# Routed rows gathered by an adding indirect DMA straight into the residual, eight groups ahead

## What is computed

```
x = x + _L0_xattn_ref(_layernorm(x), ctx, W, b)
x = x + _L0_ffn_ref(_layernorm(x), gate_w, shared and routed weights)
x = x + _L1_xattn_ref(_layernorm(x), ctx, ctx, Wq, bq, Wk, bk, Wv, bv)
x = x + _L1_ffn_ref(_layernorm(x), W_in, b_in, W_out)
```

```
top_id = jnp.argmax(x @ gate_w); score = jax.nn.sigmoid(top_val)
y = silu((x*score) @ rt_gate[e]) * ((x*score) @ rt_up[e]) @ rt_down[e]
routed = y of expert top_id;     return shared + routed
```

## Time and profile before

| | us |
|---|---|
| median of 3 runs | 897.83 |
| lowest and highest | 892.91, 898.03 |
| span of the profiled execution | 890.3 |
| TensorE busy in it | 821.5 |
| VectorE busy | 650.6 |
| ScalarE busy | 545.3 |
| GpSimd busy | 250.1 |

### The profile page before, as it was taken

One profiled execution on the slowest core, in us unless ns is written; L12 is line 12 of the kernel. 1 busy time (PEld: TensorE's weight loads), 2 busy tenths in 40 slices (PEclk: granted clock), 3 DMA queues, 4 the chain that ended last, 5 costly groups with the idle time before them and its releaser, 6 DMA issues.

```text
span 890.3 us, 15056 instructions
## 1 busy us (share of the span) xinstructions
PE 821.5 (92%) x4236; PEld 618.0 (69%) x4277; DVE 650.6 (73%) x1695; ACT 545.3 (61%) x947; POOL 250.1 (28%) x328
## 2 busy tenths in 40 slices
PE   4899998887589969999999999999999999999997
PEld 2677776666556746667777777777777777777775
DVE  3677778876574326587788888878887888788774
ACT  2365566555333313536777777787877687777765
POOL 1112112177717725012033213321321232131000
PEclk9899999999799989999999999999999999999999
DMA  5236575453235424210000000000000000000000
GB/s 143 58 93 166 157 212 154 126 143 112 81 93 154 133 74 121 71 47 22 4 25 24 18 6 24 24 7 17 24 24 0 24 24 24 0 24 13 13 1 24
DMA packets 91421, 55.66 MB, mean 63 GB/s; under 512 B 13439, under 2 KB 88183, under 8 KB 91255
## 3 DMA queue, kind: packets, MB, share of 16 engines
q1 hardware_dynamic: 74304, 40.38, 16.1%
q0 software_dynamic: 4096, 8.40, 3.3%
q10 hardware_dynamic: 12983, 6.41, 2.5%
HBM read 32.10 MB, written 23.07 MB: 62 GB/s over the span
## 4 chain that ended last, share of the span: by engine, by line
PE 62%; POOL 10%; DVE 9%; issue 7%; ACT 6%; DMA 3%; ACTq 1%; another core or an unknown queue 1%; DVEq 0%; POOLq 0%; SPq 0%
PE PS L742 7%; PE PS L987 7%; PE PS L1009 6%; PE PS L1011 6%; PE PS L1010 6%; PE PS L988 6%; PE PS L989 6%; POOL x_sorted L497 5%; PE PS L998 4%; PE PS L760 3%; POOL rs L482 2%; PE PS L996 2%; PE PS L923 2%; POOL xs L490 2%; DVE xn L1069 2%
## 5 line engine op out<-in xcount | busy, mean ns | idle before, releaser
L697 ACT ACTIVATE sil<-PS,b_in_c 128x512 f32<-128x512 f32 x256 | 161.9, 684 | 112.4 <-PE PS L996 68.1
L1374 DVE TENSOR_TENSOR sil_l<-sil,sil_h 128x512 fp32r<-128x512 f32 x256 | 164.7, 684 | 44.9 <-ACT sil_h L705 44.2
L480 POOL TENSOR_TENSOR ve<-mv,eps 128x4 f32<-128x4 f32 x64 | 17.3, 271 | 504.8 <-DVE mv L1063 504.7
L705 ACT ACTIVATE sil_h<-sil 128x512 fp32r<-128x512 f32 x224 | 128.9, 631 | 0.0
L1009 PE MATMUL PS<-sil_h,wout_l 128*128 128x512 f32 x256 | 121.4, 474 | 1.7 <-DVE sil_l L1374 1.7
L1358 DVE TENSOR_SCALAR dec<-PS,b_in_c 128x512 bf16<-128x512 f32 x128 | 95.4, 745 | 25.3 <-PE PS L989 25.3
L987 PE MATMUL PS<-x4T_h,win_l 128*128 128x512 f32 x256 | 102.5, 400 | 0.9 <-ACT sil L697 0.4
L1011 PE MATMUL PS<-sil_h,wout_h 128*128 128x512 f32 x256 | 100.6, 393 | 0.0
L1010 PE MATMUL PS<-sil_l,wout_h 128*128 128x512 f32 x256 | 100.5, 393 | 0.0
L988 PE MATMUL PS<-x4T_l,win_h 128*128 128x512 f32 x256 | 99.8, 390 | 0.0
L989 PE MATMUL PS<-x4T_h,win_h 128*128 128x512 f32 x256 | 99.8, 390 | 0.0
(11 more groups left out here) (146 smaller groups left out, 1615.8 us busy)
## 6 DMA issues: line engine op xcount, KB each, us to landing
x_sorted<-zeros SPq DMA_DIRECT2D x4, 1280.0 KB, 7.2
xs_in<-x_sorted SPq DMA_DIRECT2D x20, 256.0 KB, 3.0
y_sorted<-yo ACTq DMA_DIRECT2D x20, 256.0 KB, 2.3
X<-in_x SPq DMA_DIRECT2D x16, 256.0 KB, 6.5
rows<-xn SPq DMA_DIRECT2D x16, 256.0 KB, 2.5
xs<-rows SPq DMA_DIRECT2D x16, 256.0 KB, 3.2
out<-res SPq DMA_DIRECT2D x16, 256.0 KB, 2.4
ctxT<-in_ctx_t SPq DMA_DIRECT2D x16, 240.0 KB, 5.1
```

What stands on the lines that cost most here:

```text
L697: act.activation(tile(sil[p % 2], c, W), bank(2 * (p % 2) + c), ACT.Silu, bias=b_in_c[:, 2 * p + c:2 * p + c + 1]).then_inc(t_silu, 1)
L705: act.activation(tile(sil_h[p % 2], c, W), tile(sil[p % 2], c, W), ACT.Copy).then_inc(t_hi, 1)
L1374: dve.tensor_tensor(tile(sil_l[p % 2], c, W), tile(sil[p % 2], c, W), tile(sil_h[p % 2], c, W).bitcast(F32), ALU.subtract).then_inc(t_lo, 1)
```

## The change

Four edits belong together.

- The gather's DMA now adds (`compute_op=ALU.add`) the rows of `y_sorted` to the columns of X in SBUF, and does not copy them into `ys`.
- With that go the buffers `ys`, VectorE's addition, and the semaphore c_x2. `c_stats3` waits for the gather's own semaphore `y_in` instead.
- The DMA takes its row numbers straight from POS, so the copy to `idx` in front of each gather goes, with the wait for it (c_idx).
- The gathers need no free buffer any more, and their order on GpSimd is new. Gathers 0 to 7 (first half of `y_sorted`) are issued in stage R, and pass g issues gather g + 8. Each gather from the third on first waits until the gather two before it has landed (`y_in` of its parity), and the first one waits for all additions of stage A to X (s_add). GpSimd's passes are written out and no longer a loop.

```diff
-            def gather(h, u, half):
-                pool.tensor_copy(idx[:, u, :], cols(POS, h * G, G)).then_inc(c_idx, 1)
-                pool.wait_ge(c_idx, h + 1)
+            def gather(h):
+                u, half = h % 2, h // HG
+                if h > 1:
+                    pool.wait_ge(y_in[u], 16 * G * (h // 2))
                 pool.sem_inc(pool_passed, 1)
                 for j in range(G):
-                    pool.indirect_dma_start(tile(ys[u], j), None, y_sorted[half],
-                                            bass.IndirectOffsetOnAxis(ap=idx[:, u, j:j + 1], axis=0)
-                                            ).then_inc(y_in[u], 16)
+                    at = h * G + j
+                    pool.indirect_dma_start(X[:, at * P:(at + 1) * P], None, y_sorted[half],
+                                            bass.IndirectOffsetOnAxis(ap=POS[:, at:at + 1], axis=0),
+                                            compute_op=ALU.add).then_inc(y_in[u], 16)
...
-            gather(0, 0, 0)
-            gather(1, 1, 0)
+            pool.wait_ge(s_add, NG)
+            gather(0)
+            gather(1)
             rstd(0, 0, c_mv3, c_ve3, c_rs3)
-            gather(2, 0, 0)
+            gather(2)
+            gather(3)
             rstd(1, 0, c_mv4, c_ve4, c_rs4)
             rstd(0, 1, c_mv3, c_ve3, c_rs3)
+            for h in range(4, HG):
+                gather(h)
             for u in range(2):
                 pool.wait_ge(r_out[u], 16 * (NR // 2 + 1))
...
-                if not last(g, 2):
+                if g + 2 < NG:
                     rstd(0, g + 2, c_mv3, c_ve3, c_rs3)
-                    if not last(g, 3):
-                        gather(g + 3, 1 - u, half)
+                    if g + HG < NG:
+                        gather(g + HG)
...
-            def c_add_routed(h, u):
+            def c_stats3(h, u):
                 dve.wait_ge(y_in[u], 16 * G * (h // 2 + 1))
-                row = cols(X, h * W, W)
-                dve.tensor_tensor(row, row, ys[u], ALU.add).then_inc(c_x2, 1)
-
-            def c_stats3(h):
-                dve.wait_ge(c_x2, h + 1)
                 stats(0, h, c_st3, c_mv3)
...
-                        if p == 0:
-                            c_add_routed(g + 2, u)
                         if p == 2:
-                            c_stats3(g + 2)
+                            c_stats3(g + 2, u)
```

More of the change, by code:

```diff
@@ L211, in program @@
         yo = cut.two("yo", W)
-        ys = cut.two("ys", W)
         xn_c = cut.take("xn_c", W)
@@ L257, in program @@
         y_in, stored = sems("y_in", 2), sems("stored", 2)
-        (c_idx, c_x2, c_st3, c_mv3, c_ve3, c_rs3, c_xn3, c_xnT_ps, c_xnT, c_qT_ps, c_qT, c_s_ps, c_max, c_shift, c_exp,
+        (c_st3, c_mv3, c_ve3, c_rs3, c_xn3, c_xnT_ps, c_xnT, c_qT_ps, c_qT, c_s_ps, c_max, c_shift, c_exp,
          c_sum, c_pT_ps, c_pT, c_pv_ps, c_rec, c_x3, c_st4, c_mv4, c_ve4, c_rs4, c_xn4, c_x4T_ps, c_x4h, c_x4l) = (
              sem(n) for n in (
-                 "c_idx", "c_x2", "c_st3", "c_mv3", "c_ve3", "c_rs3", "c_xn3", "c_xnT_ps", "c_xnT", "c_qT_ps", "c_qT",
+                 "c_st3", "c_mv3", "c_ve3", "c_rs3", "c_xn3", "c_xnT_ps", "c_xnT", "c_qT_ps", "c_qT",
                  "c_s_ps", "c_max", "c_shift", "c_exp", "c_sum", "c_pT_ps", "c_pT", "c_pv_ps", "c_rec", "c_x3", "c_st4",
@@ L540, in _, with c_body @@
                 pool.wait_ge(r_out[u], 16 * (HR // 2 + 1))
-            gather(0, 0, 0)
-            gather(1, 1, 0)
+            pool.wait_ge(s_add, NG)
+            gather(0)
+            gather(1)
             rstd(0, 0, c_mv3, c_ve3, c_rs3)
-            gather(2, 0, 0)
+            gather(2)
+            gather(3)
             rstd(1, 0, c_mv4, c_ve4, c_rs4)
             rstd(0, 1, c_mv3, c_ve3, c_rs3)
+            for h in range(4, HG):
+                gather(h)
             for u in range(2):
                 pool.wait_ge(r_out[u], 16 * (NR // 2 + 1))
-            def c_body(g, u, half):
-                if not last(g, 2):
+            def c_body(g):
+                if g + 2 < NG:
                     rstd(0, g + 2, c_mv3, c_ve3, c_rs3)
-                    if not last(g, 3):
-                        gather(g + 3, 1 - u, half)
-                if not last(g, 1):
+                    if g + HG < NG:
+                        gather(g + HG)
+                if g + 1 < NG:
                     rstd(1, g + 1, c_mv4, c_ve4, c_rs4)
[L560 to L566, removed]
+            for g in range(NG):
+                c_body(g)
         @block.scalar
@@ L1301, in r_evac_a @@
                 dve.tensor_copy(actT[v], bank(5)).then_inc(r_aT, 1)
-            def c_rows3(h):
-                c_add_routed(h, h)
-                c_stats3(h)
             def c_rows4(h):
@@ L1327, in _ @@
                 if r == FIRST_EARLY:
-                    c_rows3(0)
+                    c_stats3(0, 0)
                 if r == FIRST_EARLY + 3:
@@ L1333, in _ @@
                 if r == FIRST_EARLY + 6:
-                    c_rows3(1)
+                    c_stats3(1, 1)
                 r_half(2 * r + 1, 1)
```

## The result

| | us |
|---|---|
| kernel before, median of 5 runs | 897.22 |
| changed kernel, median of 5 runs | 905.27 (903.64 to 909.41) |
| ratio to the kernel before | 1.011, 95% interval 1.0079 to 1.0141 |
| span of the profiled execution, before and after | 890.3 and 907.6 |

The changed kernel is 1.1% slower, where I forecast no change.

The account below looks back on a forecast made before the run. TensorE, busy 92% of the span, was taken to bound the kernel. Terms -0.6 + 0.65 = 0.05 us, put on the 897.83 us median and leaning towards the lower run, gave 897.5 us, range 890 to 911.

Parts of the forecast that it names:

- the price of the adding DMA: GpSimd's time per adding gather, taken as the plain gather's, 0.94 to 1.09 us; upper bound twice the mean.
- w: Pitch in us per indirect DMA on GpSimd: 1.34 taken, bounds 1.24 and 2.48.
- 16w - 20.8: Last stage, gathers 4 to 7 before rstd(0, 2): cost of sixteen DMAs beyond their cover, 0.65 us forecast.
- the earlier result on VectorE: Last stage: claimed to move both the block's start and the point of need, leaving the sixteen-DMA term unchanged.
- 8w - 12.9: Routed stage, gathers 0 and 1 before rstd(0, 0): upper-bound wait 8w + 1.3 - 14.2, before slack.
- 8w - 13.9: Routed stage, eight DMAs before rstd(0, 0): cost after a guessed 1 us of slack, 5.9 us at w = 2.48.
- Rival A: An adding gather occupies GpSimd longer, w over 1.8: slower by over 1%, up to 923 us; chance 25%.
- The gain of 0.6 us: End of routed stage: removing group 1's addition shortens the path 0.6 us, within TensorE's 0.59 us wait for actT.
- stage C gives nothing back for VectorE's 14 additions: Last stage: additions end before ScalarE's sil_h comes, so removing them only lengthens VectorE's idle time: 0.
- the landing waits in the block: Gather 6 waiting for gather 4 to land: 0 if an adding gather lands within 6.4 us.
- rival C: Slow landing, 7.6 us: gathers 6 and 7 and gather 0's statistics wait, 3.5 us, 901 us; chance 5%.
- The rule that I had set against my choice: A reducing DMA emits two read descriptors per chunk, a copy one: speaks for w = 2.48, about 26 us more.

Follow-up runs that it names:

- twelve-block: Changed kernel with gather 7 moved out of the block into pass 0, so twelve adding DMAs stand in a row instead of sixteen: 899.46 us, ratio 1.0032.
- 24 plain DMAs: Changed kernel with plain copies instead of adding gathers, and gathers 8 and 9 also put into the block: 905.02 us, ratio 1.0102.
- half the rows adding: Changed kernel with every adding gather cut to the first 64 partitions: 900.62 us in one run.
- the additions alone: Kernel before with VectorE's 16 additions left out, routed rows fetched but never added, all else the same: 895.95 us, ratio 1.0004.

## Why the prediction was wrong

**The step that failed** is the price of the adding DMA. I wrote that I take the value of the plain gather, since scatter and gather cost the same and 128 rows stay 128 rows: w = 1.34. It was 1.85 between starts (1.54 + 0.30), in the block 1.88 with its slower pieces. That scatter and gather agree says nothing about a third form. The chances followed the same step, with 25% for w over 1.8.

**The terms around the price.** For the block of sixteen the formula 16w - 20.8 gives 8.8 us at w = 1.85; TensorE's gap was 7.94. Most of the difference comes from a sentence of the prediction, that the earlier result on VectorE moves both the start of the block and the point of need. It moved only the start. rs of rstd(0, 1) came 9.27 us ahead of the first tree decision and 8.42 before the change, since group 1's statistics no longer stand behind an addition; VectorE asked for rs of rstd(0, 2) 13.3 us behind that decision, and 13.2 before. The twelve-block moved VectorE's wait by 7.36 us, by the formula 7.4.

In stage R two errors nearly cancel. Before any slack, the prediction's terms make VectorE's wait 8w - 12.9, which is 1.9 us; it was 4.11. The eight DMAs took 15.3 us and not 14.5, as one of them took 2.16 us; gather 0 began hardly earlier without its copy (5.9 us ahead of the first rounding of tree weights, and 5.8 before), where I had moved it forward by 0.8 us; and VectorE, without its addition, asked about 0.7 us sooner. But TensorE lost only 1.7 us of it, so the slack there was over 2 us and not the 1 that I had guessed. That 8w - 13.9 gives 0.9 us for these 1.7 is therefore no test of it.

Rival A's own sum with w = 1.85 is 9.7 us and 907 us. That this lies close to the 905.27 measured is partly luck: it counts the gap 0.9 us too high and stage R 0.8 too low, and it lacks the next term.

**A term was missing.** After a stall of 7.94 us TensorE's first 3.96 us of work ran at the lower clock, 1.8 us more. Behind 8.46 us (24 plain DMAs) it was 2.3 us more, behind 5.46 us (half the rows adding) 1.4, behind 0.55 us nothing.

**The gain of 0.6 us** for the addition in stage R is nothing: a gap of 0.59 or 0.60 us stayed in all traces with no addition. I had followed VectorE's busy stretch to TensorE's gap without asking for what VectorE waited in between. It is small in the sum, but it is the only gain that I had claimed.

**What was right:** that stage C gives nothing back for VectorE's 14 additions (474.8 us with them, 474.9 without), that the copies of POS are worth nothing (the plain gathers in the new order run without them, and 0.9988 with an interval of 0.9966 to 1.0009 is no gain that can be told from none), that the landing waits in the block are covered (GpSimd shows no more than the usual 0.30 us in front of gathers 6 and 7), and that four DMAs between two rstd fit. An adding gather lands 3.2 to 4.7 us after its issue (in the old order), under the 6.4 that I had left it; rival C did not come.

**The rule that I had set against my choice** (the Trainium skill, Collectives: The Full Stack, "Why ReduceScatter is half of AllGather") pointed the right way and too far. Two read descriptors where a copy has one would make w = 2.48 if GpSimd's whole time doubled with them. What was measured lies between that and no surcharge: 1.5 times in the mean (1.09 to 1.65 us), 1.6 times for the shortest (0.94 to 1.53). The cut rows speak against a time that goes by how much is read: with half the rows an adding DMA still takes 1.40 of its 1.53 us. Whether an adding DMA has twice the read descriptors, no run here shows.

## What to carry to other kernels

An engine that issues DMAs in order pays for each of them, and its idle time in front of a small instruction that others wait for is a budget: count the DMAs between two such instructions, times their pitch. When an operation changes its form (a copy that now adds), don't take the old form's price; ask if the budget still holds at one and a half times, the ratio measured here. Here the work that left VectorE, which is not the bound, gave nothing back by itself (the additions alone, above), so it wasn't worth a denser stretch on GpSimd.

## What the runs showed of the hardware

- An indirect DMA that adds holds GpSimd for 1.53 us at the shortest and 1.65 in the mean, the plain one for 0.94 and 1.09. By the estimate above the surplus is mostly fixed (0.42 of 0.59 us) and a little by rows; half the bytes changed nothing. The packets of its queue rise from 4,096 to 11,264 for the same 8.40 MB: the 64 scatters are the same in both, so the 64 gathers took 7,168 packets more, 112 each. Of an adding gather's packets one goes with each row (64 rows fewer, 64 packets fewer), whatever the row's bytes.
- Landing takes 3.2 us from issue at the shortest and 3.5 in the median (old order, adding), where the plain gather of the kernel before has 2.5 and 2.9.
- TensorE's clock was at the lower level behind gaps of 5.46, 7.94 and 8.46 us, for the first 2.8, 4.0 and 5.2 us of work, and at the upper one behind a gap of 0.55 us. Stalls of this size cost about a quarter more than their length (1.4, 1.8 and 2.3 us).
